# A logits stage reordered: the third user group alone for 11 strips, the two last groups together for 14, the last group alone for 11, with the last group's sums and dense pieces 39 blocks sooner

## The chip, the core and the metric

The program runs on one core of one Trainium2 chip. The metric is the device time of one execution in microseconds (us). One execution has also been recorded by the hardware profiler; its rows are shown below.

## What is computed

Embeddings of 200 items per user are pooled, 50 retrieved rows per user are averaged, both go through small dense layers, and the fused vector of each of the 1,024 users is multiplied with a projection of 12,500 items.

```python
seq_emb = jnp.where(mask, item_embeddings[clip(sequence_ids - 1, 0)], 0.0)
pooled = seq_emb.sum(axis=1) / denom
user_rep = pooled @ W_rec.T + b_rec                              # 512 wide
retrieved = item_embeddings[retrieved_indices].mean(axis=1)      # 50 rows of each user
gate = jax.nn.sigmoid(concat([user_rep, retrieved]) @ gate_W.T + gate_b)
fused = gate * user_rep + (1.0 - gate) * retrieved
logits = fused @ proj_W.T + proj_b                               # 1024 x 12500
```

## The kernel before, in words

**Groups, strips, blocks.** The 1,024 users are four groups (0 to 3) of 512, each four blocks of 128. The 12,500 items are NS = 25 strips of W = 500. A block of logits (128 users by 500 items) is made by `make_logits` with 12 matmuls (four of the hidden dimension's slices, times three products of high and low f16 parts), each 128 by 500, into one of BANKS = 5 banks. VectorE (DVE) evicts it at L955 into `rows` (the profile's `ring`), with the scale from `out_scale` and the bias; ScalarE (ACT) issues the store of every four blocks. `rows` holds three such sets of four.

**The logits stage.** It is a list STEPS of 400 blocks, and each engine walks through it in its own program order. A *turn* is one load of a strip. For each turn SyncE (SP) loads the strip (1 MB, `load_strip`) and its bias row spread over the partitions (`load_bias`, 250 KB), ACT makes the high part (`high_strip`, L1114), DVE the low part (`low_strip`, L772), and `scale_out` makes the combined scale (L780). Turns 0 to 24 use groups 0 and 1 (8 blocks a turn, 200 blocks). Turns 25 to 49 load all strips again for group 2 (4 blocks a turn, blocks 200 to 299), and turns 50 to 74 again for group 3 (blocks 300 to 399). TensorE (PE) waits for `strip_low` at the first block of a turn, and for `fused_low` of the group. A strip's squares and sum (L1105, L1316) and its scale are made once, in the first 25 turns. A turn's high and low parts are made at the turn before it: at its blocks 3 and 4 if that turn has 8 blocks, at its blocks 0 and 1 if it has 4.

**The dense work of groups 2 and 3** is threaded into the same walk by a table of block numbers, `LOGITS`. For a group there are `pool` (the pooled vector comes in and is split), 12 `pieces` on PE (four USER of 12 matmuls, L1238; four TURN, transposes of the retrieved means, L1256; four GATE of 24 matmuls), `square` and `sum` (a common scale), `high`, `low`, `diff`, `mix` (the gate is applied, in two steps at `mix` and `mix + 1`), `fsum` (the fused vector's scale; PE L1298) and `flow` (its low part, DVE L759, the last thing needed before the group's first logits).

**The gathers.** GpSimd (POOL) gathers the retrieved rows of 128 users with indirect DMAs (L560) into 11 slots of two gathers; DVE adds a slot's two gathers at L726 (`add_batch`), which frees the slot. There are 288 such adds, 114 before the logits stage. The other 174 are spread over blocks 5 to `ADDS_END` in proportion to PE's matmuls there (12 for a block, plus those of the dense pieces). When a block of users is summed POOL stores it (L565), and when all four of group 3 are there it loads them back for the transposes (`load_ret`, L614). TURN of group 3 waits for that load.

```python
block_work = accumulate(3 * KH + products(LOGITS, n) if n > LOGITS[1]["flow"] else 0 for n in range(ADDS_END + 1))
def adds_by_block(n):
    first, last = ADDS_PASS[NG - 1], len(pl.adds)
    return first if n < 0 else first + (last - first) * block_work[min(n, ADDS_END)] // block_work[-1]
```

Of the kernel before, what the change touches and what calls it, by code (L numbers as in the profile page):

```python
# [16 lines left out]
P = 128  # L17
# [15 lines left out]
ROWS = 4  # L33
# [27 lines left out]
    3: dict(pool=172, pieces=(174, 176, 178, 180, 256, 257, 258, 259, 269, 271, 273, 275), square=261, sum=263, high=264,  # L61
            low=266, diff=268, mix=277, fsum=283, flow=285),
# [9 lines left out]
ADDS_END = 246  # L72
# [72 lines left out]
def pooling_program(nc, pl, ids, ret_ids, emb, w_rec_t, b_rec, w_gate_t, b_gate, proj_t, proj_b,  # L145
# [9 lines left out]
    LAST = len(STEPS)  # L155

    def ended(t):

        return 1 + max(n for n, (turn, j) in enumerate(STEPS) if turn <= t)


    strip_steps = {"square": {9: 2}, "sum": {10: 2}, "high": {12: 2}, "low": {12: 2}}
    for t in range(3, TURNS):
        begun = STEPS.index((t - 1, 0))
        if t < NS:
            strip_steps["square"][begun] = t
            strip_steps["sum"][begun + 2] = t
# [3 lines left out]
    def group_of_step(t, j):  # L171
        return j // GROUP_BLOCKS if t < NS else t // NS + 1

    with ExitStack() as scope:
# [258 lines left out]
        def _(sp):  # L433
# [32 lines left out]
            def load_strip(t):  # L466
                c = t % NS
                if t >= 2:
                    sp.wait_ge(strip_low, t - 1)
                sp.dma_start(strip[:, t % 2], proj[:, :, c * W:(c + 1) * W]).then_inc(strip_in[t % 2], 16)  # L470

            def load_bias(t):
                c = t % NS
# [179 lines left out]
        def _(dve):  # L653
# [115 lines left out]
            def low_strip(t):  # L769
                c = t % NS  # L770
# [4 lines left out]
            def scale_out(t, groups=None):  # L775
                c = t % NS
                first, last = groups or ((0, 2) if t < NS else (t // NS + 1, t // NS + 2))
                at = first if t < NS else 0
# [165 lines left out]
            scale_out(0, (0, 1))  # L944
            scale_out(1, (0, 1))
            dve.drain()

            for n, (t, j) in enumerate(STEPS):
# [3 lines left out]
                if j == 0:  # L952
                    dve.wait_ge(bias_in[t % 2], 16 * (t // 2 + 1))
                dve.wait_ge(logits_made, n + 1)
                dve.scalar_tensor_tensor(rows[:, r % ROW_SLOTS, v], logit_ps[n % BANKS][:, 0:W],  # L955
                                         out_scale[:, t % 2, j // GROUP_BLOCKS:j // GROUP_BLOCKS + 1], bias[:, t % 2],
# [3 lines left out]
                if n in strip_steps["low"]:  # L960
                    made = strip_steps["low"][n]
                    low_strip(made)
                    if made % NS > 0:
                        scale_out(made)
                        dve.drain()
                dense_scales(n, LOGITS)
                dense_parts(n, LOGITS)
                if n == LOGITS[1]["flow"]:
                    scale_out(0, (1, 2))
                    scale_out(1, (1, 2))  # L970
# [3 lines left out]
                if t + 1 in (NS, 2 * NS) and n + 1 == ended(t):  # L974
                    dve.drain()
                    scale_out(t + 1)
                    dve.drain()
# [3 lines left out]
        def _(act):  # L981
# [126 lines left out]
            def high_strip(t):  # L1108
                c = t % NS
# [7 lines left out]
            def store_rows(r):  # L1117
                t, j = STEPS[r * ROWS]
                c = t % NS
                first = group_of_step(t, j) * GROUP_BLOCKS  # L1120
# [4 lines left out]
            def store_last_rows(v):  # L1125

                act.wait_ge(logits_moved, LAST - ROWS + v + 1)
                act.dma_start(out.rearrange("(b p) i -> p b i", p=P)[:, pl.blocks - ROWS + v, (NS - 1) * W:],
                             rows[:, (LAST // ROWS - 1) % ROW_SLOTS, v]).then_inc(last_stored, 16)

# [41 lines left out]
            for n, (t, j) in enumerate(STEPS):  # L1172
# [15 lines left out]
        def _(pe):  # L1188
# [130 lines left out]
            def make_logits(n):  # L1319
                t, j = STEPS[n]  # L1320
                g = group_of_step(t, j)
                if j == 0:
                    pe.wait_ge(strip_low, t + 1)
                if j % GROUP_BLOCKS == 0:
# [5 lines left out]
                at_user = (g % 2 * GROUP_BLOCKS + j % GROUP_BLOCKS) * P  # L1330
# [32 lines left out]
            for n, (t, j) in enumerate(STEPS):  # L1363
# [66 lines left out]
```

## Time and profile before

| | |
|---|---|
| device time, three runs | 2155.1, 2154.89, 2150.67 us; median 2154.89 |
| span of the profiled execution | 2152.5 us |
| PE, DVE, ACT, POOL busy over the span | 96%, 74%, 38%, 52% |
| stretch from 980 us to the end: PE idle | 10.3 of 1,172 us (1161.67 busy) |
| granted TensorE clock in that stretch | 1.00 |
| DMA share in 1600 to 1700 us, and in 2000 to 2100 us | 0.99 (356 GB/s), 0.68 (227 GB/s) |

No device time is given for the profiled execution by itself, only its span; the median of the runs is 2.4 us above it. Busy times are per engine. Idle time of an engine counts only where another waits for it. A "busy" of a stretch is the sum of the instructions' spans inside it. An ordinary gap between two DVE instructions (some 0.1 to 0.2 us) is not counted as busy.

### The profile page before, as it was taken

Reading aid. Unit: us, or ns where it says so; the run is one execution under the profiler, and the core shown is the slowest. Engines: PE = TensorE matmul, PEld = TensorE weight load, DVE = VectorE, ACT = ScalarE, POOL = GpSimd, SP = SyncE. Lnnn points to the kernel's source line nnn. Section 1 sums busy time; section 2 is a strip of 40 time slices with the busy share of each in tenths; the row PEclk is TensorE's granted clock in tenths of the full one; section 3 lists DMA queues with packets and bytes.
Section 4 is the critical chain, followed back from the end, with each engine's and each line's share of the span. In section 5 each row is a group of like instructions: output and inputs, shape, how many; then the busy total and the mean of one; then the engine's idle time right before and its main releaser. Section 6 shows DMA issues by size and latency. Waiting matters only on the chain.

```text
span 2152.5 us, 32020 instructions
## 1 busy us (share of the span) xinstructions
PE 2066.9 (96%) x12722; PEld 1060.7 (49%) x12722; DVE 1599.5 (74%) x1837; ACT 818.2 (38%) x1009; POOL 1117.7 (52%) x830
## 2 busy tenths in 40 slices
PE   5679999999999999999999999999999999999999
PEld 4555555555555554444444444444444444444444
DVE  8999999888888886444577787787878865655554
ACT  5866676444544455435211212232211222212111
POOL 5574552788678855656366666657667600000000
PEclk9559999999999999999999999999999999999999
DMA  8999997999899987979589998878899975566665
GB/s 300 339 230 302 289 324 253 308 250 258 240 272 246 250 296 254 322 245 330 176 281 335 317 307 300 297 266 267 318 318 350 370 237 170 196 223 235 229 218 187
DMA packets 222050, 586.82 MB, mean 273 GB/s; under 512 B 21840, under 2 KB 121040, under 8 KB 218576
## 3 DMA queue, kind: packets, MB, share of 16 engines
q1 hardware_dynamic: 91424, 264.21, 36.1%
q0 software_dynamic: 77632, 218.16, 35.8%
q10 hardware_dynamic: 52848, 102.41, 12.7%
q8 instruction: 103, 1.69, 0.3%
q14 instruction: 43, 0.35, 0.0%
HBM read 448.21 MB, written 136.48 MB: 272 GB/s over the span
## 4 chain that ended last, share of the span: by engine, by line
PE 85%; DVE 8%; ACT 3%; DVEq 1%; issue 1%; DMA 1%; another core or an unknown queue 0%; POOL 0%; ACTq 0%; SPq 0%; POOLq 0%
PE pooled_ps L1333 36%; PE pooled_ps L1226 27%; PE count_ps L1333 9%; PE count_ps L1208 7%; PE count_ps L1238 6%; DVE row_hots L681 2%; ACT counts L991 2%; DVE keys L683 2%; DVE recip L698 1%; ACT counts L985 1%; DMA mid<-emb 0%; DVEq L725 0%; DMA row_hots<-ret_dram 0%; DVE ring L688 0%; PE count_ps L1256 0%
## 5 line engine op out<-in xcount | busy, mean ns | idle before, releaser
L1226 PE MATMUL pooled_ps<-mid,ring 128*128 128x512 f16 x3136 | 725.4, 379 | 3.8 <-ACT mid L1009 1.9
L560 POOL DMA_INDIRECT gathered<-emb,ret_rows x460 | 556.1, 1209 | 308.4 <-DVE gathered L726 144.4
L1226 PEld LDWEIGHTS pooled_ps<-mid,ring 128*128 128x128 f16 x3136 | 292.3, 98 | 309.9 <-issue 4.5
L1333 PE MATMUL pooled_ps<-counts,mid 128*128 128x500 f16 x1920 | 413.0, 374 | 1.0 <-DVE counts L772 0.9
L1333 PE MATMUL pooled_ps<-counts,keys 128*128 128x500 f16 x1920 | 413.9, 374 | 0.0
L582 POOL DMA_INDIRECT gathered<-emb,ret_rows x184 | 342.4, 1861 | 132.7 <-ACT ring L999 56.3
L955 DVE SCALAR_TENSOR_TENSOR ring<-pooled_ps,out_scale,counts 128x500 f32<-128x500 f32 x320 | 234.3, 736 | 223.9 <-PE pooled_ps L1333 199.8
L681 DVE TENSOR_TENSOR row_hots<-pair_columns,keys 128x2048 f16<-128x2048 f16 x256 | 312.8, 1222 | 70.3 <-PE count_ps L1208 57.8
L1114 ACT ACTIVATE counts<-counts,strip_scale 128x2000 f16<-128x2000 f32 x75 | 147.0, 1960 | 509.2 <-PE pooled_ps L1333 291.3
L1208 PE MATMUL count_ps<-keys,row_hots 128*128 128x98 f16 x4096 | 280.5, 224 | 59.7 <-DVE keys L683 42.6
L1208 PEld LDWEIGHTS count_ps<-keys,row_hots 128*128 128x128 f16 x4096 | 250.1, 107 | 139.1 <-DVE keys L683 59.4
L985 ACT ACTIVATE counts<-count_ps 128x392 uint8<-128x392 f32 x512 | 237.9, 491 | 201.4 <-PE count_ps L1208 177.9
L1333 PEld LDWEIGHTS pooled_ps<-counts,mid 128*128 128x128 f16 x1920 | 186.6, 97 | 218.9 <-DVE counts L772 1.7
L1333 PEld LDWEIGHTS pooled_ps<-counts,keys 128*128 128x128 f16 x1920 | 185.1, 97 | 215.5
L1009 ACT ACTIVATE mid<-counts 128x1024 f16<-128x1024 uint8 x196 | 205.8, 1054 | 163.6 <-PE pooled_ps L1226 129.6
L683 DVE TENSOR_TENSOR keys<-pair_columns,keys 128x1568 f16<-128x1568 f16 x256 | 247.9, 968 | 0.0
L726 DVE TENSOR_TENSOR gathered<-gathered 128x1024 f32<-128x1024 f32 x159 | 195.0, 1226 | 57.9 <-issue 19.0
L772 DVE SCALAR_TENSOR_TENSOR counts<-counts,strip_scale 128x2000 f16<-128x2000 f32 x75 | 172.0, 2294 | 6.3 <-ACT counts L1114 6.3
L560 POOL DMA_INDIRECT counts<-emb,ret_rows x108 | 136.2, 1262 | 56.9 <-issue 30.2
L1333 PE MATMUL count_ps<-counts,keys 128*128 128x500 f16 x480 | 107.8, 374 | 0.0
L1333 PE MATMUL count_ps<-counts,mid 128*128 128x500 f16 x480 | 107.8, 374 | 0.0
L955 DVE SCALAR_TENSOR_TENSOR ring<-count_ps,out_scale,counts 128x500 f32<-128x500 f32 x80 | 58.9, 736 | 52.8 <-PE count_ps L1333 42.0
(134 smaller groups left out, 1110.6 us busy)
## 6 DMA issues: line engine op xcount, KB each, us to landing
logits<-ring ACTq DMA_DIRECT2D x99, 1000.0 KB
ring<-emb_parts SPq DMA_DIRECT2D x147, 512.0 KB
counts<-proj_t SPq DMA_DIRECT2D x75, 1000.0 KB
counts<-emb SPq DMA_DIRECT2D x14, 1792.0 KB, 10.9
emb_parts<-ring SPq DMA_DIRECT2D x49, 512.0 KB, 8.5
mid<-emb SPq DMA_DIRECT2D x46, 512.0 KB
counts<-proj_b SPq DMA_DIRECT2D x75, 250.0 KB
gathered<-emb,ret_rows POOLq DMA_INDIRECT x660
```

What stands on the lines that cost most here:

```text
L560: pool.indirect_dma_start(slots[group][:, a], None, source, column(block, r * SLOT + a))\
L582: pool.indirect_dma_start(to, None, source, column(block, n), compute_op=ALU.add).then_inc(landed, 16)
L681: dve.tensor_tensor(row_hots[:, n % 2], cols.broadcast_to((P, 8, P, 2)), rk.broadcast_to((P, 8, P, 2)), ALU.is_equal)
L683: dve.tensor_tensor(chunk_hots[:, n % 2], cols[:, :, 0:NQ].broadcast_to((P, 8, NQ, 2)), ck.broadcast_to((P, 8, NQ, 2)), ALU.is_equal).then ...
L726: dve.tensor_tensor(slots[total], slots[total], slots[more], ALU.add).then_inc(added, 1)
L772: dve.scalar_tensor_tensor(strip_parts[:, t % 2, 1], strip[:, t % 2], strip_scale[:, c:c + 1], strip_parts[:, t % 2, 0], ALU.mult, ALU.sub ...
L955: dve.scalar_tensor_tensor(rows[:, r % ROW_SLOTS, v], logit_ps[n % BANKS][:, 0:W], out_scale[:, t % 2, j // GROUP_BLOCKS:j // GROUP_BLOCKS ...
L985: act.activation(counts_v[:, g % 2, :, k * QUAD:(k + 1) * QUAD], count_ps[:, q % COUNT_BANKS, 0:QUAD * NQ].rearrange("p (u c) -> p c u", u ...
L1009: act.activation(cvt[:, p % CVT], counts_v[:, g % 2, 2 * i:2 * i + 2], ACT.Copy).then_inc(cvt_made, 1)
L1208: last = pe.matmul(to, row_hots[:, slot, pair * 2 + part, :, v], chunk_hots[:, slot, pair * 2 + part, :, v], start=(part == 0), stop=(part ...
L1226: last = pe.matmul(pooled_ps[:, m], ring_v[:, p % RING, c, part, m * P:(m + 1) * P], cvt[:, p % CVT, c], start=(i == 0 and c == 0 and part ...
L1333: last = pe.matmul(logit_ps[n % BANKS][:, 0:W], fused[g // 2][:, f, k, at_user:at_user + P], strip_parts[:, t % 2, w, k, :], start=(k == 0 ...
```

## The change

Group 3 no longer has 25 turns of its own behind those of group 2. Strips 0 to 10 are loaded for group 2 alone (11 turns of 4 blocks, blocks 200 to 243), strips 11 to 24 for groups 2 and 3 together (14 turns of 8 blocks, 244 to 355), and strips 0 to 10 again for group 3 alone (11 turns of 4 blocks, 356 to 399). There are 61 turns in place of 75, and still 400 blocks of 12 matmuls. The first block of group 3 is 248 in place of 300. So group 3's TURN and GATE pieces and everything behind them move 39 blocks to the front (`flow` from 285 to 246), its `pool` and USER pieces stay, and the adds end at block 207 in place of 246. `out_scale` of turn 36 for group 3 is made behind `flow`.

```diff
-    3: dict(pool=172, pieces=(174, 176, 178, 180, 256, 257, 258, 259, 269, 271, 273, 275), square=261, sum=263, high=264,
-            low=266, diff=268, mix=277, fsum=283, flow=285),
+    3: dict(pool=172, pieces=(174, 176, 178, 180, 217, 218, 219, 220, 230, 232, 234, 236), square=222, sum=224, high=225,
+            low=227, diff=229, mix=238, fsum=244, flow=246),
-ADDS_END = 246
+ADDS_END = 207
+ALONE = 11
-    TURNS = 3 * NS
-    STEPS = [(t, half * GROUP_BLOCKS + j) for half in range(2) for t in range(2) for j in range(GROUP_BLOCKS)]
-    STEPS += [(t, j) for t in range(2, TURNS) for j in range(2 * GROUP_BLOCKS if t < NS else GROUP_BLOCKS)]
+    LOADS = [(c, (0, 1)) for c in range(NS)] + [(c, (2,)) for c in range(ALONE)]
+    LOADS += [(c, (2, 3)) for c in range(ALONE, NS)] + [(c, (3,)) for c in range(ALONE)]
+    TURNS = len(LOADS)
+    STEPS = [(t, g, b) for g in range(2) for t in range(2) for b in range(GROUP_BLOCKS)]
+    STEPS += [(t, g, b) for t in range(2, TURNS) for g in LOADS[t][1] for b in range(GROUP_BLOCKS)]
...
-        strip_steps["high"][begun + (3 if t <= NS else 0)] = t
-        strip_steps["low"][begun + (4 if t <= NS else 1)] = t
+        wide = len(LOADS[t - 1][1]) > 1
+        strip_steps["high"][begun(t - 1) + (3 if wide else 0)] = t
+        strip_steps["low"][begun(t - 1) + (4 if wide else 1)] = t
...
-                    if made % NS > 0:
-                        scale_out(made)
-                        dve.drain()
+                    ready = [group for group in LOADS[made][1] if group == 0 or LOGITS[group]["flow"] < n]
+                    scale_out(made, ready[0], ready[-1] + 1)
+                    dve.drain()
...
+                if n == LOGITS[3]["flow"]:
+                    for made in range(NS, TURNS):
+                        if low_at[made] <= n < ended(made) and 3 in LOADS[made][1]:
+                            scale_out(made, 3, 4)
+                    dve.drain()
```

The rest of the diff carries the strip and the group of each step (`LOADS[t][0]`, `g`) into the loads, the stores, `high_strip`, `low_strip` and `make_logits`.

## Rows read from the trace of the kernel before

**Rows 1.** The page: busy time of each engine, share of the span, instructions.
```profile
PE 2066.9 (96%) x12722; PEld 1060.7 (49%) x12722; DVE 1599.5 (74%) x1837; ACT 818.2 (38%) x1009; POOL 1117.7 (52%) x830
```

**Rows 2.** Windows: length, busy us (count) of each engine, clock, DMA share, GB/s.
```profile
1130.00:1340.00 210.00, 210.00 (x1005) 96.81 (x1004) 165.32 (x249) 43.11 (x32) 138.11 (x120) 1.00 0.92 318
1380.00:1535.00 155.00, 152.98 (x738) 70.90 (x736) 124.33 (x184) 40.40 (x35) 104.91 (x88) 1.00 0.86 297
1600.00:1712.00 112.00, 112.00 (x533) 51.61 (x531) 91.75 (x95) 20.41 (x11) 83.09 (x63) 1.00 0.99 357
1870.00:2140.00 270.00, 270.00 (x1280) 124.46 (x1279) 144.24 (x161) 51.01 (x26) 0.00 (x0) 1.00 0.67 224
```

**Rows 3.** The chain that ended last: start, length, engine, tile, line, count.
```profile
1721.22 10.13 PE pooled_ps L1333 x48
...
2139.16 10.15 PE pooled_ps L1333 x48
```

**Rows 4.** Waits of PE from 980 us: us in total, times, longest.
```profile
PE count_ps L1238 <- DVE counts L801: 2.5, 2, 1.6
PE spare_ps L1316 <- issue: 1.4, 1, 1.4
PE count_ps L1238 <- DVE keys L823: 1.3, 1, 1.3
PE pooled_ps L1333 <- DVE counts L772: 0.9, 1, 0.9
...
PE count_ps L1256 <- DMA row_hots<-ret_dram: 0.7, 1, 0.7
```

**Rows 5.** Groups of instructions from 980 us: busy us, mean ns | idle before, releaser.
```profile
L955 DVE SCALAR_TENSOR_TENSOR ring<-pooled_ps,out_scale,counts 128x500 f32<-128x500 f32 x320 | 234.3, 736 | 223.9 <-PE pooled_ps L1333 199.8 <-issue 13.5 <-remote 7.0
...
L772 DVE SCALAR_TENSOR_TENSOR counts<-counts,strip_scale 128x2000 f16<-128x2000 f32 x75 | 172.0, 2294 | 6.3 <-ACT counts L1114 6.3
L1114 ACT ACTIVATE counts<-counts,strip_scale 128x2000 f16<-128x2000 f32 x75 | 147.0, 1960 | 509.2 <-PE pooled_ps L1333 291.3 <-issue 110.6 <-PE count_ps L1333 56.9
```

**Rows 6.** Timeline at the end of group 2's dense work: start, us, engine, line.
```profile
1491.50 0.16 PE L1316 MATMUL spare_ps<-strip_sq,ones_f 128*128 128x1 bf16 x1 [1.36 <-issue]
...
1501.99 2.29 DVE L772 SCALAR_TENSOR_TENSOR counts<-counts,strip_scale 128x2000 f16<-128x2000 f32 x1
1504.34 2.71 PE L1333 MATMUL count_ps<-counts,keys 128*128 128x500 f16 x12
```

**Rows 7.** POOL's groups in 1600 to 1712 us, columns as in rows 5.
```profile
L560 POOL DMA_INDIRECT gathered<-emb,ret_rows x38 | 49.5, 1302 | 17.4 <-issue 10.4 <-DVE gathered L726 7.0
L560 POOL DMA_INDIRECT counts<-emb,ret_rows x24 | 34.3, 1429 | 11.4 <-issue 7.0 <-DVE gathered L726 4.4
```

**Rows 8.** Timeline: last gather, last add, load of the sums, group 3's first TURN.
```profile
1710.52 1.06 POOL L560 DMA_INDIRECT counts<-emb,ret_rows  x1 [0.30 <-issue]
...
1739.29 1.22 DVE L726 TENSOR_TENSOR gathered<-gathered,counts 128x1024 f32<-128x1024 f32 x1
...
1745.72 0.56 POOL L614 DMA_DIRECT2D row_hots<-ret_dram  x1 [3.54 <-DMA ret_dram<-gathered]
...
1761.59 0.60 PE L1256 MATMUL count_ps<-identity,row_hots 128*128 128x128 f32 x4
```

**Rows 9.** Timeline from group 3's last GATE piece to its fused low part.
```profile
1834.78 10.30 PE L1333 MATMUL pooled_ps<-counts,mid 128*128 128x500 f16 x48
...
1837.62 0.74 DVE L955 SCALAR_TENSOR_TENSOR ring<-pooled_ps,out_scale,counts 128x500 f32<-128x500 f32 x1 [7.07 <-PE pooled_ps L1333]
...
1846.67 2.29 DVE L745 TENSOR_TENSOR counts<-counts 128x2048 f32<-128x2048 f32 x1
...
1849.00 1.91 ACT L1067 ACTIVATE counts<-counts 128x2048 f32<-128x2048 f32 x1 [11.39 <-DVE counts L745]
...
1852.89 2.30 DVE L772 SCALAR_TENSOR_TENSOR counts<-counts,strip_scale 128x2000 f16<-128x2000 f32 x1 [1.97 <-ACT counts L1114]
...
1865.45 2.35 DVE L759 SCALAR_TENSOR_TENSOR mid<-counts,fused_scale,mid 128x2048 f16<-128x2048 f32 x1
```

More of the change, by code:

```diff
@@ L150, in pooling_program, with begun @@
     GROUP_BLOCKS = G // P
-    TURNS = 3 * NS
-    STEPS = [(t, half * GROUP_BLOCKS + j) for half in range(2) for t in range(2) for j in range(GROUP_BLOCKS)]
-    STEPS += [(t, j) for t in range(2, TURNS) for j in range(2 * GROUP_BLOCKS if t < NS else GROUP_BLOCKS)]
+    LOADS = [(c, (0, 1)) for c in range(NS)] + [(c, (2,)) for c in range(ALONE)]
[3 more added lines that the diff above has]
+    STEPS += [(t, g, b) for t in range(2, TURNS) for g in LOADS[t][1] for b in range(GROUP_BLOCKS)]
     LAST = len(STEPS)
+    def begun(t):
+        return min(n for n, step in enumerate(STEPS) if step[0] == t)
     def ended(t):
-        return 1 + max(n for n, (turn, j) in enumerate(STEPS) if turn <= t)
+        return 1 + max(n for n, step in enumerate(STEPS) if step[0] <= t)
     strip_steps = {"square": {9: 2}, "sum": {10: 2}, "high": {12: 2}, "low": {12: 2}}
     for t in range(3, TURNS):
-        begun = STEPS.index((t - 1, 0))
         if t < NS:
-            strip_steps["square"][begun] = t
-            strip_steps["sum"][begun + 2] = t
-        strip_steps["high"][begun + (3 if t <= NS else 0)] = t
-        strip_steps["low"][begun + (4 if t <= NS else 1)] = t
-    def group_of_step(t, j):
-        return j // GROUP_BLOCKS if t < NS else t // NS + 1
+            strip_steps["square"][begun(t - 1)] = t
+            strip_steps["sum"][begun(t - 1) + 2] = t
+        wide = len(LOADS[t - 1][1]) > 1
+        strip_steps["high"][begun(t - 1) + (3 if wide else 0)] = t
+        strip_steps["low"][begun(t - 1) + (4 if wide else 1)] = t
+    low_at = {t: n for n, t in strip_steps["low"].items()}
     with ExitStack() as scope:
@@ L773, in low_strip, with scale_out @@
                                          strip_parts[:, t % 2, 0], ALU.mult, ALU.subtract).then_inc(strip_low, 1)
[L775 to L778, printed above, removed]
+            def scale_out(t, first, last):
+                c, at = LOADS[t][0], first - LOADS[t][1][0]
                 dve.drain()
@@ L943, in _ @@
             dve.drain()
-            scale_out(0, (0, 1))
-            scale_out(1, (0, 1))
+            scale_out(0, 0, 1)
+            scale_out(1, 0, 1)
             dve.drain()
-            for n, (t, j) in enumerate(STEPS):
+            for n, (t, g, b) in enumerate(STEPS):
                 r, v = divmod(n, ROWS)
@@ L955, in _ @@
                 dve.scalar_tensor_tensor(rows[:, r % ROW_SLOTS, v], logit_ps[n % BANKS][:, 0:W],
-                                         out_scale[:, t % 2, j // GROUP_BLOCKS:j // GROUP_BLOCKS + 1], bias[:, t % 2],
+                                         out_scale[:, t % 2, g - LOADS[t][1][0]:g - LOADS[t][1][0] + 1], bias[:, t % 2],
                                          ALU.mult, ALU.add).then_inc(logits_moved, 1)
@@ L968, in _ @@
                 if n == LOGITS[1]["flow"]:
-                    scale_out(0, (1, 2))
-                    scale_out(1, (1, 2))
+                    scale_out(0, 1, 2)
+                    scale_out(1, 1, 2)
+                    dve.drain()
[3 more added lines that the diff above has]
+                            scale_out(made, 3, 4)
                     dve.drain()
@@ L973, in _ @@
                     add_batch(k)
[L974 to L977, printed above, removed]
         @block0.scalar
@@ L1117, in store_rows @@
             def store_rows(r):
-                t, j = STEPS[r * ROWS]
-                c = t % NS
-                first = group_of_step(t, j) * GROUP_BLOCKS
+                t, g, b = STEPS[r * ROWS]
+                c = LOADS[t][0]
+                first = g * GROUP_BLOCKS
                 act.wait_ge(logits_moved, ROWS * (r + 1))
@@ L1127, in store_last_rows @@
                 act.wait_ge(logits_moved, LAST - ROWS + v + 1)
-                act.dma_start(out.rearrange("(b p) i -> p b i", p=P)[:, pl.blocks - ROWS + v, (NS - 1) * W:],
+                act.dma_start(out.rearrange("(b p) i -> p b i", p=P)[:, pl.blocks - ROWS + v, (ALONE - 1) * W:ALONE * W],
                              rows[:, (LAST // ROWS - 1) % ROW_SLOTS, v]).then_inc(last_stored, 16)
@@ L1171, in _ @@
                                 high_strip(c)
-            for n, (t, j) in enumerate(STEPS):
+            for n in range(LAST):
                 if n in strip_steps["square"]:
@@ L1362, in _ @@
                                 sum_strip(c)
-            for n, (t, j) in enumerate(STEPS):
+            for n in range(LAST):
                 make_logits(n)
```

19 lines of the change are left out of this document (9 added, 10 removed).

## The prediction

> **What bounds the kernel now.** I read the page first: PE is busy for 96% of the span, all others far less [rows 1]. That alone doesn't say that PE sets the end in the stage that is changed, so the windows come next. The granted clock is 1.00 in each, its upper level (2.4 GHz) [rows 2]. Read in them how PE's busy time stands to the length: 210.00 of 210, 112.00 of 112, 270.00 of 270 [rows 2]. The logits stage is matmuls back to back. The chain of waits says the same: it is PE L1333 in runs of 48 matmuls, 10.13 us for four blocks at 1721 us and 10.15 at the very end [rows 3]. One block is 2.53 us, one matmul 0.211. The two runs lie in different company, the first in the time of a DMA share near 0.99, the second at 0.67 [rows 2]. So a block costs the same under a full and under a half-empty DMA system. Last I read who makes PE wait: five lines, 6.8 us together [rows 4]. This is the whole of what any reordering of this stage can win, unless it removes matmuls. The change keeps 400 blocks of 12 and all 24 moved pieces.
>
> **What is taken away.** 14 turns go: each an `high_strip` on ACT (1.96 us), a `low_strip` on DVE (2.29), a small `scale_out`, a 1 MB load and a 250 KB bias. That is 27 us of ACT and 32 us of DVE [rows 5] and 17.5 MB. The cover is plain: in 1870 to 2140 us, with a turn every four blocks, DVE is busy for 144 us of 270 and ACT for 51, while PE is never idle [rows 2]. DVE waited for PE at the eviction for 199.8 us [rows 5]. The transfers are hidden as well, since a strip is asked for one turn and more ahead. Worth 0. All of this relief lies behind block 244; nothing of it helps the stretch ahead of it, which gets denser.
>
> **Adds closer together.** 174 adds are laid over PE's matmuls in blocks 5 to ADDS_END. Before: 242 blocks of 12, group 2's pieces 160, group 3's USER 48, 3,112 in all, or 17.9 matmuls an add, 3.77 us. After: 203 blocks, 2,644, or 15.2 matmuls, 3.21 us. Over 155 us that is 7.2 more adds, each 1.22 us [rows 8] and some 0.1 of gap, 9.5 us of DVE. In the densest stretch, 1380 to 1535, DVE is busy for 124.3 of 155 us [rows 2]; 30.7 are free, though some 18 of them are ordinary gaps between its 184 instructions. So DVE doesn't become the bound on average. Locally it does:
> - Group 2's end. L772 of block 156 ends at 1504.29 and PE's block 160 begins at 1504.34 [rows 6]: that low part is just in time. DVE has no rest between `mix` (147) and this point. By the formula of `adds_by_block` 6 adds stand in blocks 147 to 155 before, 7 after. One add more is 1.3 us of lateness, straight onto PE. It shows either at block 160 or already at block 154, where the strip's sum waits for `fused_scaled` for 1.36 us [rows 6], since that wait and the later one are on one DVE sequence: count it once. +1.3, bounds 0 (a gap takes it) and 2.6 (two adds).
> - Group 2's GATE at 139 waits for `both_low` in the same way: 3 adds in blocks 131 to 135 before, 4 after. The trace shows no wait there, but the margin is under a block. +0.3, bounds 0 and 1.3.
> - The TURN of group 2 waited 0.7 us for its rows [rows 4]. The adds that they need end at block 103 in place of 117, so this goes: -0.7.
>
> **The gathers.** They must all be in 39 blocks, 99 us, earlier. POOL now needs two per 3.21 us, 1.60 us each. In its slowest stretch 62 gathers took 83.8 us and 17.4 of issue, 1.63 us each, with 11.4 us of waiting for adds beside it [rows 7]; in 1130 to 1340 it is busy for 138 us with 120 instructions, 1.15 each, some 1.45 with the same 0.28 of issue [rows 2]. The slow stretch has the DMA share at 0.99, the other at 0.92. After the change all gathers lie in the cheaper kind but for the last few: with 8-block turns the strips, biases and stores are 3.33 MB in 20.3 us, 164 GB/s, and the gathers 0.524 MB in 3.21 us, 163 GB/s. 327 GB/s is asked where 357 were moved [rows 2]. POOL is then used to 90%. Its lead covers the rest: the last gather is issued at 1711.6 and the last add begins at 1739.3 [rows 8], 27.7 us. 0.
>
> The Trainium skill (DMA: Bandwidth & Descriptors, Specifications) gives a core some 358 GB/s of HBM bandwidth, which speaks against this packing. The slow stretch agrees with its 357. By that page the 8 blocks from 200 to 207, where short turns (227 GB/s) and gathers meet at 390, would fall behind by 32 GB/s for 20 us, 0.6 MB, an estimate of 2 us of transfer; as all of it is prefetch the sum would stay as it is.
>
> **Group 3's rows come back in time.** Add, store, load: 1739.3 to 1745.7, and PE's TURN at 1761.59 with no wait [rows 8, 4]. The last add (207) and the TURN (217) stay ten blocks apart. The store and the load stand last in POOL's queue, so nothing waits behind them. 15.3 us from the load's issue to the TURN held 1 MB under rising traffic; an add that is 3 us late changes nothing. 0.
>
> **Group 3's dense work.** It is the same chain with turn boundaries (multiples of 4) one block nearer. Before, `high_strip` stood behind `high_both` at block 264 and delayed `low_strip`: PE waited 0.9 for a strip and 1.3 for `both_low` [rows 4]. After, `high_strip` is at 224 and `high_both` at 225: both waits go, -2.2. What comes later is tighter, though. Take the start of the block behind the last GATE (276 before, 237 after) as zero. Before, evictions began at 2.84, the second mix at 11.9 and `square_fused` at 14.2, the strip's low part ended at 20.4, and its turn (284) began 8 blocks and a sum behind zero, 20.5 [rows 9]: in time by nothing. After: eviction 2.8 to 3.6, low part 5.9, first mix to 9.4, second to 12.8, `square_fused` to 15.0, high part 17.0, low part 19.3; but the turn (244) begins at 7 blocks, 17.7. PE waits 1.6. Then `fsum` at 244: PE ends that block at 21.9, eviction and scale to 24.6, high part 26.7, eviction 246 to 28.0, `low_fused` (2.35 us) to 30.4; block 248 can begin at 29.7. PE waits 0.7. Together +2.3, bounds 0 (DVE runs ahead) and 4.9, the case that `low_fused` ends 7.5 us behind its block as it does before (1867.8 [rows 9]; block 285 ends ten blocks and a sum behind zero, at 1860.3), with block 248 only 2.5 us away. Net with the two waits that go: +0.1.
>
> **Sum.** +1.3 +0.3 -0.7 +0.1 = +1.0 us. Span 2153.5; with the 2.4 us by which the median of the runs is above the span, 2155.9. I say 2156.
>
> **Rivals.**
> - DVE falls behind in group 2's stretch. For: DVE's small slack between blocks 131 and 160, and 7 adds more there. Against: it waits for PE again at several evictions, and five banks give 10 us. If the free time in 1380 to 1535 turned out to be all gaps, each added add would count in full: +9.5 us, 2164. It decides once DVE is late by four blocks, or a turn's low part by more than 3 us.
> - The gathers come late, and DVE stops in an add with evictions queued behind it. Each gather would have to cost over 1.60 + 27.7/348 = 1.68 us; the slowest stretch had 1.63. At 1.75 it is 348 times 0.07, +24 us: 2180.
> - The waits vanish: groups 2 and 3 both without a stall and none new. All 6.8 us won, 2148. Against: three of the five waits sit at places that the change leaves alone.
> - PE's matmuls get nearer together once DVE and DMA have less to do, that is behind block 244. At 1% of 156 blocks it would be 4 us, 2152 or below. Against: 10.13 and 10.15 us in unlike company. The Trainium skill (TensorE: Matmul & The Clock Gate, Back-to-back issue gap) has a sustained spacing of about 131 ns for 512 columns, by which 211 ns would not be PE's floor; this trace disagrees, with 48 matmuls in 10.13 us in every stretch.
> - The change doesn't do what it says: the turns do go, so it would be the gain that is absent, and this is my forecast.
>
> **How the numbers follow.** The forecast (small waits traded) 0.72; DVE short 0.13; gathers late 0.05; waits vanish 0.05; nearer matmuls 0.02; something not listed 0.03, taken as slower. 0.2% is 4.3 us, about what this kernel's runs differ by (2150.67 to 2155.1). The forecast's own bounds are 2153 to 2160 with unlike executions allowed for; 2159.2 is already "slower", some 0.01 of it, and as much goes to faster. Faster: the vanished waits 0.05, the nearer matmuls 0.02, a low draw of the forecast 0.01, together 0.08. Slower: DVE short 0.09 (its other 0.04 costs under 4 us), the late gathers 0.05, the unlisted 0.03, a high draw 0.01, together 0.18. Same: the rest, 0.74. The range is 2150 (half the waits won, low draws) to 2164 (DVE short in full); the late gathers and the full gain are left out.
>
> **What would show it.** Right: PE busy for all but some 10 us from 980 us on, still 10.13 us per four blocks, DVE busy for less behind block 244, POOL's last gather near 1612 us and the last add near 1640, and short waits at blocks 160, 244 and 248. Wrong: PE waits with `rows` or `logits_moved` behind it (an eviction, L955) between 1400 and 1520 us; DVE idle ahead of L726; a TURN at some 1663 us that waits for the load; a block that costs other than 2.53 us.

## The result and the profile after

The kernel with the change takes 2171.1 us (median of four runs, 2166.72 to 2173.71); the kernel before took 2152.78 beside it (four runs, 2149.57 to 2155.1). The ratio is 1.0085, 95% interval 1.0072 to 1.0097. It is some 18 us slower, and the forecast (2156, range 2150 to 2164) was wrong. The profiled execution has a span of 2170.2 us and a time of its own of 2171.93.

The page of the kernel after: busy time of each engine, and who sets the end, by engine. It answers to [rows 1].

```profile
PE 2072.6 (96%) x12722; PEld 1063.2 (49%) x12722; DVE 1564.4 (72%) x1810; ACT 789.9 (36%) x995; POOL 1156.2 (53%) x830
...
PE 53%; POOL 26%; DVE 7%; issue 6%; DMA 3%; ACT 3%; DVEq 1%; ACTq 0%; POOLq 0%; SPq 0%
```

PE's matmuls are the same 12,722, with 5.7 us more of busy time. DVE and ACT lose 35 and 28 us, as the 14 dropped turns should have it. POOL's 830 instructions are the same as before and take 38.5 us more. That is the first odd number: nothing in the diff makes a gather larger.

The end of the chain of waits after, and windows after (columns as in [rows 2]):

```profile
2156.78 10.15 PE pooled_ps L1338 x48
```

```profile
1300.00:1400.00 100.00, 90.74 (x418) 40.81 (x417) 73.64 (x103) 20.59 (x17) 81.10 (x65) 0.95 0.91 309
...
1500.00:1600.00 100.00, 91.92 (x426) 41.44 (x427) 77.34 (x107) 22.60 (x18) 78.87 (x64) 0.97 0.90 309
...
1900.00:2000.00 100.00, 100.00 (x476) 46.06 (x475) 41.30 (x50) 9.81 (x5) 0.00 (x0) 1.00 0.48 165
```

Four blocks still end in 10.15 us, as in [rows 3], and from 1900 to 2000 us PE is never idle at full clock while DVE is busy for 41 us and the DMA share is 0.48. The part that the change lightened costs what it did. Most of the loss lies in two hundreds, 1300 to 1400 and 1500 to 1600 us, where PE is idle for 9.3 and 8.1 us (before 2.3 and 0.9) and the clock's mean is below 1.

PE's waits after, from 980 us on (total, times, longest), against [rows 4]:

```profile
PE count_ps L1244 <- DVE counts L806: 14.0, 2, 8.4
PE pooled_ps L1338 <- DVE counts L779: 3.8, 4, 1.8
PE spare_ps L1322 <- DVEq L759: 2.1, 1, 2.1
PE spare_ps L1304 <- ACT counts L1073: 1.2, 2, 1.0
PE pooled_ps L1338 <- DVE mid L766: 0.6, 1, 0.6
...
PE count_ps L1262 <- DMA row_hots<-ret_dram: 0.4, 1, 0.4
```

(Lines are shifted: L801 of before is L806, L772 is L779, L1238 is L1244, L1333 is L1338, L955 is L960, L726 is L733, L560 is L567.) After, they sum to 22.1 us, of which the 0.4 for `row_hots` lies ahead of the logits stage. Before it is 7.7 and not the 6.8 of [rows 4], which leaves out two small ones:

```profile
PE count_ps L1238 <- issue: 0.7, 2, 0.4
...
PE spare_ps L1298 <- ACT counts L1067: 0.2, 1, 0.2
```

Two of the waits after make 14.0: the first USER piece of group 2 (block 110) and that of group 3 (block 174) wait for the low part of the pooled vector, L806, for 8.42 and 5.60 us. Ahead of the result that line was only the largest of PE's small waits. Of the 3.8 us at L779, 3.0 are low parts of strips that are late in the same way (at 1323, 1536 and 1666 us), and they are gone where the gathers are healed, in the run with one input below; 0.8 are at block 244.

Each of the two idle times at L806 is followed by a second cost. PE in the timeline after, the same piece of group 2 before, and the windows of the two pieces after:

```profile
1349.59 5.28 PE L1244 MATMUL count_ps<-counts 128*128 128x512 f16 x12 [8.42 <-DVE counts L806]
...
1559.33 4.91 PE L1244 MATMUL count_ps<-counts 128*128 128x512 f16 x12 [5.60 <-DVE counts L806]
```

```profile
1344.57 2.75 PE L1238 MATMUL count_ps<-counts 128*128 128x512 f16 x12 [1.61 <-DVE counts L801]
```

```profile
1349.60:1354.80 5.20, 5.20 (x13) 1.84 (x14) 4.90 (x5) 0.00 (x0) 4.29 (x5) 0.50 0.90 297
1559.40:1564.10 4.70, 4.70 (x13) 1.66 (x14) 4.52 (x5) 0.00 (x0) 3.62 (x4) 0.54 0.88 309
```

The granted clock is 0.50 and 0.54 over these pieces, so 1.2 GHz, its lower level, for nearly all of them; twelve such matmuls take 5.28 and 4.91 us where the piece before, at 2.4 GHz, took 2.75. That is 4.7 us for both.

**The account.** The stage goes from the first block (1049.35 before, 1047.63 after) to the end of the last four (2139.16 + 10.15 and 2156.78 + 10.15). Its windows, before and after:

```profile
1049.35:2149.31 1099.96, 1092.32 (x5199) 503.40 (x5197) 756.46 (x979) 236.87 (x168) 435.62 (x363) 1.00 0.79 270
```

```profile
1047.63:2166.93 1119.30, 1097.45 (x5199) 504.45 (x5197) 720.06 (x951) 209.63 (x154) 470.34 (x363) 0.99 0.73 249
```

It is 19.3 us longer: PE is idle for 14.2 us more (21.85 for 7.64), and busy for 5.1 more, of which the two slow pieces are 4.7. The stage began 1.7 us sooner, which leaves +17.7 on the span.

**Why the low part is late.** What DVE waits for in 1100 to 1660 us, DMA rows only:

```profile
DVE gathered L733 <- DMA gathered<-emb,ret_rows: 18.0, 16, 2.4
...
DVE gathered L733 <- DMA counts<-emb,ret_rows: 7.3, 5, 3.9
...
DVE counts L733 <- DMA counts<-emb,ret_rows: 4.4, 2, 3.7
...
DVE counts L733 <- DMA gathered<-emb,ret_rows: 1.8, 2, 1.0
```

The adds stop for gathered rows for 31.5 us, and everything behind them in DVE's queue stops with them. Around block 109 DVE's evictions are 12.2 us behind PE's blocks. PE bridges that as long as a bank is free; a low part in the same queue has no such cushion. So the gathers come late. POOL's groups in 1100 to 1600 us, after and then before:

```profile
L567 POOL DMA_INDIRECT gathered<-emb,ret_rows x215 | 280.9, 1307 | 66.7 <-issue 64.3 <-DMA ret_dram<-gathered 2.1 <-DVE counts L733 0.3
L567 POOL DMA_INDIRECT counts<-emb,ret_rows x90 | 119.5, 1327 | 30.0 <-issue 26.8 <-DMA ret_dram<-counts 2.9 <-DVE counts L733 0.3
```

```profile
L560 POOL DMA_INDIRECT gathered<-emb,ret_rows x196 | 234.0, 1194 | 122.9 <-issue 49.6 <-DVE gathered L726 44.4 <-DVE counts L726 27.8
L560 POOL DMA_INDIRECT counts<-emb,ret_rows x78 | 96.3, 1234 | 43.7 <-issue 21.3 <-DVE gathered L726 16.4 <-DVE counts L726 6.0
```

Before, POOL waits for adds for 94.6 us of these 500 (44.4 + 27.8 + 16.4 + 6.0): it is ahead and is held back. After, it waits for them for 0.6 us. It issues without a rest, 305 gathers in 280.9 + 119.5 + 66.7 + 30.0 = 497.1 us, or 1.63 us each. POOL is busy for 53% of the span on the page and for 400.4 us of these 500, and is their bound all the same: nearly all of the rest is the 0.30 us of issue between two gathers.

**What makes a gather dear** shows in the timeline, POOL and DVE together:

```profile
1335.86 0.95 POOL L567 DMA_INDIRECT gathered<-emb,ret_rows  x1 [0.30 <-issue]
1336.72 1.22 DVE L733 TENSOR_TENSOR counts<-counts 128x1024 f32<-128x1024 f32 x1 [3.65 <-DMA counts<-emb,ret_rows]
1337.11 1.65 POOL L567 DMA_INDIRECT gathered<-emb,ret_rows  x1 [0.30 <-issue]
...
1340.32 0.95 POOL L567 DMA_INDIRECT gathered<-emb,ret_rows  x1 [0.30 <-issue]
...
1340.64 1.22 DVE L733 TENSOR_TENSOR counts<-counts,gathered 128x1024 f32<-128x1024 f32 x1 [0.18 <-issue]
...
1344.40 2.29 DVE L779 SCALAR_TENSOR_TENSOR counts<-counts,strip_scale 128x2000 f16<-128x2000 f32 x1
1344.96 2.55 POOL L567 DMA_INDIRECT counts<-emb,ret_rows  x1 [0.30 <-issue]
...
1347.09 2.35 DVE L806 SCALAR_TENSOR_TENSOR counts<-counts,small 128x2048 f16<-128x2048 f32 x1
1347.81 2.44 POOL L567 DMA_INDIRECT counts<-emb,ret_rows  x1 [0.30 <-issue]
```

A gather takes 0.95 us while DVE waits. One that begins while an add is running (1337.11) ends 0.82 us behind the add's end, and takes 1.65; one that is already under way when the add begins (1340.32) still takes 0.95. Those that begin under the two low parts take 2.55 and 2.44. Add and low part are DVE instructions that read two inputs from SBUF.

The trace of 1100 to 1600 us says the same of all gathers, once the start of each is laid over these DVE instructions. Of 304 gathers 177 begin while one runs; they take 1.58 us in the mean, and 166 of them end 0.8 us behind it. The other 127 take 0.95, none over 1.0. Among these are 45 that begin during an eviction, which reads one input from SBUF and writes 500 columns. Before, 110 of 273 begin under a two-input instruction, again at 1.58 us, and the other 163 take 0.95. Call such a gather caught: its price didn't change; the share of caught ones did, from 40% to 58%. Two things go with it. The adds come every 3.21 us in place of 3.77. And POOL no longer waits: before, 52 gathers had waited for an add to free their slot, so that they began behind its end, and 2 of them were caught; of the other 221 it was 49%.

**How much was asked of POOL.** Here the working before the result has a miscount, and the section on the gathers ahead of it has it too. An add doesn't join the two gathers of a slot: it adds a slot of two rows to the total, and 50 rows are 25 slots and 24 adds, the first slot being the total itself. (That section also says 1,024 users; there are 2,048, four groups of 512, and the 288 adds are those of 12 blocks of 128.) The 174 adds need 174 × 25/24 × 2 = 362 gathers (359 of them are in the trace after), not 348. So the pace asked is 3.21/2.083 = 1.54 us a gather, not 1.60. At 1087 to 1260 us the trace has 104 gathers, 1.66 us each, where 112 were due: four slots short. Counted back from the last gather and the last add, POOL's lead is 7 slots at 1087 us and between 2 and 3 at 1260 (within a slot, since a few records are missing); before, it is between 6 and 9 all the way. From then on the adds wait.

### The profile page after: what moved, and what is told of

It is laid out like the page before. It is cut to its first block, busy times and chain, and to the rows that moved or that the text cites. A ratio compares the mean times of both kernels' runs of the same rounds, so it can differ in the third digit from the quotient of the medians.

```text
span 2170.2 us, 31909 instructions
## 1 busy us (share of the span) xinstructions
PE 2072.6 (96%) x12722; PEld 1063.2 (49%) x12722; DVE 1564.4 (72%) x1810; ACT 789.9 (36%) x995; POOL 1156.2 (53%) x830
## 4 chain that ended last, share of the span: by engine, by line
PE 53%; POOL 26%; DVE 7%; issue 6%; DMA 3%; ACT 3%; DVEq 1%; ACTq 0%; POOLq 0%; SPq 0%
PE pooled_ps L1232 22%; PE pooled_ps L1338 17%; POOL gathered L567 16%; POOL counts L567 6%; PE count_ps L1214 6%; PE count_ps L1338 4%; POOL gathered L589 3%; PE count_ps L1244 3%; ACT counts L997 2%; DVE row_hots L688 2%; DVE keys L690 1%; DMA ret_dram<-gathered 1%; DMA counts<-pool_dram 1%; ACT counts L991 1%; DMA ret_dram<-counts 0%
## 5 line engine op out<-in xcount | busy, mean ns | idle before, releaser
L567 POOL DMA_INDIRECT gathered<-emb,ret_rows x460 | 585.1, 1272 | 239.2 <-issue 133.2
L589 POOL DMA_INDIRECT gathered<-emb,ret_rows x184 | 349.7, 1901 | 127.5 <-ACT ring L1005 55.3
L1338 PE MATMUL pooled_ps<-counts,keys 128*128 128x500 f16 x1920 | 414.8, 374 | 2.6 <-DVE counts L779 2.6
L1338 PE MATMUL pooled_ps<-counts,mid 128*128 128x500 f16 x1920 | 413.0, 374 | 1.8 <-DVE counts L779 1.2
L960 DVE SCALAR_TENSOR_TENSOR ring<-pooled_ps,out_scale,counts 128x500 f32<-128x500 f32 x320 | 235.0, 736 | 244.0 <-PE pooled_ps L1338 241.2
L1120 ACT ACTIVATE counts<-counts,strip_scale 128x2000 f16<-128x2000 f32 x61 | 119.6, 1960 | 574.4 <-DVE ring L960 242.7
L1338 PEld LDWEIGHTS pooled_ps<-counts,mid 128*128 128x128 f16 x1920 | 186.6, 97 | 220.5 <-DVE counts L779 2.2
L1338 PEld LDWEIGHTS pooled_ps<-counts,keys 128*128 128x128 f16 x1920 | 185.2, 97 | 219.2 <-DVE counts L779 3.6
L733 DVE TENSOR_TENSOR gathered<-gathered 128x1024 f32<-128x1024 f32 x159 | 194.9, 1226 | 69.0 <-PE pooled_ps L1232 35.9
L567 POOL DMA_INDIRECT counts<-emb,ret_rows x108 | 141.8, 1313 | 35.5 <-issue 32.3
L779 DVE SCALAR_TENSOR_TENSOR counts<-counts,strip_scale 128x2000 f16<-128x2000 f32 x61 | 139.9, 2294 | 5.0 <-ACT counts L1120 2.6
L1338 PE MATMUL count_ps<-counts,keys 128*128 128x500 f16 x480 | 107.8, 374 | 0.1
L1338 PE MATMUL count_ps<-counts,mid 128*128 128x500 f16 x480 | 107.8, 374 | 0.0
L1244 PE MATMUL count_ps<-counts 128*128 128x512 f16 x384 | 92.4, 393 | 14.0 <-DVE counts L806 14.0
```

The costliest lines, as they stand in the source:

```text
L567: pool.indirect_dma_start(slots[group][:, a], None, source, column(block, r * SLOT + a))\
L589: pool.indirect_dma_start(to, None, source, column(block, n), compute_op=ALU.add).then_inc(landed, 16)
L733: dve.tensor_tensor(slots[total], slots[total], slots[more], ALU.add).then_inc(added, 1)
L1244: done = pe.matmul(to, weights[:, w, k, m * P:(m + 1) * P], x, start=(first and k == 0 and at == 0), stop=(last and k == KH - 1 and at == 2))
L1338: last = pe.matmul(logit_ps[n % BANKS][:, 0:W], fused[g // 2][:, f, k, at_user:at_user + P], strip_parts[:, t % 2, w, k, :], start=(k == 0 ...
```

## Experiments

The kernels named below are the kernel before or after with one edit. Expectations were written ahead of the runs and go by the miscounted paces: their 1.60, 1.75 and 1.66 us a gather (11, 16 and 13 strips alone) are 1.54, 1.68 and 1.60 by the right count.

### The adds sooner, nothing else

The kernel before, with its own order and table.

```diff
-ADDS_END = 246
+ADDS_END = 207
```

> The kernel before with one number changed: the adds end at block 207 in place of 246. Steps, turns and dense table are those of before. Theory G (POOL can't gather at the asked pace of one per 1.60 us, so adds wait for rows, and DVE comes late to group 2's and 3's low_pool): the cost is nearly all there, 12 to 20 us over before, with PE waiting for low_pool (L801) for 10 us or more, as in the changed kernel (14.0). Rival O (the new order of turns or the moved dense table costs the time): within 3 us of before.

Measured: 2171.64 us (four runs, 2169.02 to 2177.4), 20.3 above the kernel before beside it, ratio 1.0099, interval 1.0082 to 1.0116. PE's largest wait:

```profile
PE count_ps L1238 <- DVE counts L801: 13.7, 2, 7.5
```

One number makes the whole loss, with the same wait, 13.7 us for 14.0. POOL's gathers are at 1.29 and 1.32 us and wait 0.3 us for an add in 500.

### The order, nothing else

Against the kernel before (cut):

```diff
+ALONE = 21
...
+    LOADS = [(c, (0, 1)) for c in range(NS)] + [(c, (2,)) for c in range(ALONE)]
+    LOADS += [(c, (2, 3)) for c in range(ALONE, NS)] + [(c, (3,)) for c in range(ALONE)]
```

The rest of the change is kept; `LOGITS` and `ADDS_END` are those of before, for which group 3 may begin behind strip 21 at the soonest.

> The new order of turns with the dense table and ADDS_END of before: group 2 alone for 21 strips, both for 4, group 3 alone for 21 (first block of group 3 is 288, flow stays 285). Theory G: the time of before within 3 us, PE waits under 10 us in all. Rival O: slower by 5 us or more, with PE waits behind block 284.

Measured: 2152.11 us (ten runs, 2150.18 to 2152.64), ratio 1.0002, interval 0.9993 to 1.0012. POOL waits for adds for 94 us again, and PE's waits sum to 6.4. The order costs and brings nothing.

### Adds with one input from SBUF

The test of the mechanism: the kernel after, with the 174 adds replaced by an instruction of the same length that reads the new slot alone and writes two columns. It leaves out the sums of the retrieved rows; the waits, slots and gathers stay.

```diff
-                dve.tensor_tensor(slots[total], slots[total], slots[more], ALU.add).then_inc(added, 1)
+                if k < ADDS_PASS[3]:
+                    dve.tensor_tensor(slots[total], slots[total], slots[more], ALU.add).then_inc(added, 1)
+                else:
+                    dve.tensor_reduce(slots[total][:, :, 0], slots[more], AX.X, ALU.add).then_inc(added, 1)
```

> The changed kernel, where the 174 adds of the logits stage are replaced by a tensor_reduce over the newly gathered slot alone, about 1.1 us long as the add is (1.22), but with one SBUF input in place of two; so the retrieved sums of groups 2 and 3 are left out. Waits, slots and gathers stay. Theory G with its cause (a gather's descriptors wait while DVE runs an instruction with two SBUF inputs): gathers get shorter, from a mean of 1.31 us to 1.15 or less, POOL waits for adds again, and the time is within 4 us of before. Rival D (bandwidth, or POOL's own pace): gathers keep their mean of 1.3 us and the time stays at 2165 or more.

Measured: 2153.16 us (ten runs, 2150.51 to 2155.23), ratio 1.0006, interval 0.9997 to 1.0016. Its groups in 1100 to 1600 us (L736 is the stand-in here), its window, and behind it that window of the kernel after:

```profile
L567 POOL DMA_INDIRECT gathered<-emb,ret_rows x227 | 246.7, 1087 | 102.9 <-issue 59.8 <-DVE gathered L736 25.6 <-DVE counts L736 15.3
...
L736 DVE TENSOR_REDUCE gathered<-gathered 128x2 f32<-128x1024 f32 x71 | 86.7, 1222 | 8.0 <-issue 2.4
```

```profile
1100.00:1600.00 500.00, 493.62 (x2361) 227.49 (x2360) 416.52 (x586) 113.47 (x94) 354.52 (x331) 1.00 0.92 328
```

```profile
1100.00:1600.00 500.00, 480.13 (x2271) 219.83 (x2269) 399.36 (x562) 110.31 (x92) 403.64 (x313) 0.98 0.91 312
```

The stand-in takes 1222 ns, as the adds do (1225). The order, the table and the pace are those of the change. DVE is busy for longer than in the kernel after (416.52 us for 399.36) and the DMA engines move more (328 GB/s for 312). The second input is gone, and with it the loss: a gather takes 1.09 us, POOL waits for adds again (58.5 us), and 323 gathers in 500 us are 1.55 us each, which is the pace asked. PE's waits are 7.9 us. So it is neither DVE's load nor the memory's, and not the moved dense work either.

The edit takes away most of what an add writes as well (2 columns for 1,024). That this is not the cause is seen beside it: the 45 gathers that begin during an eviction, with one input from SBUF and 500 columns written, take 0.95 us in the kernel after. The 117 that begin under a stand-in take 0.95 too, where one that began under an add took up to 2 us. In this kernel 34 of 322 gathers are still caught, by the low parts and the other two-input instructions of the dense work.

The Trainium skill (SBUF — State Buffer, "SBUF: two separate sides" and "Who interferes with whom") has a DVE instruction with two SBUF inputs contend with a GpSimd instruction that reads SBUF, and one with a single SBUF input, outside the 2-port modes, not. The trace and this run agree, with 1.31 against 1.09 us. The Trainium skill adds, in the second of these sections, that in a probe `tensor_tensor` didn't stall a DMA; for these indirect gathers the timeline above disagrees (1.65 us for one that begins under an add, 0.95 without).

### Half of the stores' traffic

The rival that memory traffic slows the gathers. The kernel after, with half of each row of logits left unstored (but for the last four blocks).

```diff
-                act.dma_start(out.rearrange("(b p) i -> p b i", p=P)[:, first:first + ROWS, c * W:(c + 1) * W],
-                             rows[:, r % ROW_SLOTS]).then_inc(rows_stored[r % ROW_SLOTS], 16)
+                act.dma_start(out.rearrange("(b p) i -> p b i", p=P)[:, first:first + ROWS, c * W:c * W + W // 2],
+                             rows[:, r % ROW_SLOTS, :, 0:W // 2]).then_inc(rows_stored[r % ROW_SLOTS], 16)
```

> The changed kernel, where each store of four blocks of logits but the last carries the first 250 of its 500 columns (the others are left out), so that in the 8-block turns some 50 GB/s of some 325 go. All instructions stay. Theory G with its cause: the gathers' mean stays near 1.3 us and the time near that of the changed kernel, 2165 or more. Rival D (DMA bandwidth makes the gathers late): the waits of the adds shrink and the time goes to 2158 or less.

Measured: 2166.61 us (four runs, 2163.51 to 2168.01), ratio 1.0069, interval 1.0054 to 1.0083. In 1100 to 1600 us:

```profile
L567 POOL DMA_INDIRECT gathered<-emb,ret_rows x217 | 283.9, 1308 | 66.1 <-issue 66.1
```

```profile
1100.00:1600.00 500.00, 487.84 (x2312) 223.80 (x2311) 406.27 (x576) 111.50 (x93) 406.36 (x315) 0.99 0.86 271
```

271 GB/s in place of 312, and a gather still takes 1308 ns (1307). Traffic isn't what makes issue dear. Beside its own kernel before it is 14.8 us slower, where the change was 18.3; the two intervals overlap, so some 3.5 us may have gone. What the trace does show is a shorter time from issue to landing. The last figure of a row is its median in us, in 1100 to 1600 us, first after, then here:

```profile
gathered<-emb,ret_rows POOLq DMA_INDIRECT x215, 6.0
```

```profile
gathered<-emb,ret_rows POOLq DMA_INDIRECT x217, 5.1
```

With a small lead the adds wait for landings, so this may be what gave the time back; no run sets it apart. It is not what healed the kernel with one input, where the median is 6.1.

### The pooled vector's parts sooner

The rival that the two low parts are only placed too late. The kernel after:

```diff
-    2: dict(pool=108, pieces=(110, 112, 114, 116, 126, 127, 128, 129, 139, 141, 143, 145), square=130, sum=132, high=133,
+    2: dict(pool=98, pieces=(110, 112, 114, 116, 126, 127, 128, 129, 139, 141, 143, 145), square=130, sum=132, high=133,
-    3: dict(pool=172, pieces=(174, 176, 178, 180, 217, 218, 219, 220, 230, 232, 234, 236), square=222, sum=224, high=225,
+    3: dict(pool=167, pieces=(174, 176, 178, 180, 217, 218, 219, 220, 230, 232, 234, 236), square=222, sum=224, high=225,
```

> The changed kernel with low_pool and high_pool of group 2 at block 98 in place of 108 and of group 3 at 167 in place of 172; the USER pieces stay. Theory G: POOL sets the pace, so the wait only moves: L806 no longer holds PE, but PE then waits at evictions or at group 3's TURN, and 8 us or more over before remain (of 18). Rival L (it is only that low_pool stands too near to its pieces): the time goes to within 4 us of before.

Measured: 2171.53 us (four runs, 2167.96 to 2175.53), ratio 1.0084, interval 1.0067 to 1.0101. Nothing is won. PE's largest waits, and DVE's for rows:

```profile
PE pooled_ps L1338 <- DVE counts L779: 10.9, 6, 3.5
...
PE spare_ps L1297 <- DVEq L774: 4.4, 1, 4.4
```

```profile
DVE gathered L733 <- DMA gathered<-emb,ret_rows: 34.5, 22, 5.6
```

The wait at the low part of the pooled vector is gone, and the strips' low parts (L779) take its place, not the evictions or group 3's TURN that were expected. The adds wait for rows for 68.8 us in all instead of 31.5 (1100 to 1660 us), and some other low part is late. The likely reason is that PE's long stop had let the gathers catch up; this was not tested by itself. Whoever reads only PE's waits mends the place, not the shortage.

### The same edit on the kernel before

```diff
-    2: dict(pool=108, pieces=(110, 112, 114, 116, 126, 127, 128, 129, 139, 141, 143, 145), square=130, sum=132, high=133,
+    2: dict(pool=104, pieces=(110, 112, 114, 116, 126, 127, 128, 129, 139, 141, 143, 145), square=130, sum=132, high=133,
-    3: dict(pool=172, pieces=(174, 176, 178, 180, 256, 257, 258, 259, 269, 271, 273, 275), square=261, sum=263, high=264,
+    3: dict(pool=169, pieces=(174, 176, 178, 180, 256, 257, 258, 259, 269, 271, 273, 275), square=261, sum=263, high=264,
```

> The kernel before with low_pool and high_pool of group 2 at block 104 in place of 108 and of group 3 at 169 in place of 172, the pieces where they are. The gathers have slack there, so PE's two waits for L801 (2.5 us) go: 1 to 3 us faster, at the edge of what can be measured. If the waits turn up elsewhere: no change.

Measured: 2147.8 us (eleven runs, 2145.53 to 2151.24), ratio 0.9981, interval 0.9972 to 0.999. Its waits of PE:

```profile
PE spare_ps L1316 <- DVEq L752: 1.4, 1, 1.4
PE count_ps L1238 <- DVE keys L823: 1.3, 1, 1.3
PE pooled_ps L1333 <- DVE counts L772: 0.9, 1, 0.9
PE spare_ps L1298 <- ACT counts L1067: 0.2, 1, 0.2
```

Where POOL has its lead the same cure works: the 2.5 us at L801 of [rows 4] are gone and not replaced. A small win, 4.0 us below the kernel before beside it, and its interval holds it apart from no change.

### 16 and 13 strips alone

How tight may it be? The kernel after, with less moved to the front: group 3's table from its TURN on is 20 or 8 blocks later than in the kernel after (the table's lines are left out of the cuts below).

```diff
-ADDS_END = 207
+ADDS_END = 227
...
-ALONE = 11
+ALONE = 16
```

> Half the shift: group 2 alone for 16 strips, both groups for 9, group 3 alone for 16; group 3's later entries of the dense table 20 blocks later than in the changed kernel (flow 266, first block 268), the adds end at block 227. They then come one per 16.6 matmuls, 3.50 us, 1.75 us a gather. Theory G: POOL manages 1.6, so the gathers keep up: within 3 us of before. Rival N (the loss grows with each block of shift, by half here): 2160 to 2163.

Measured: 2150.01 us (twelve runs, 2147.77 to 2157.74), ratio 0.9997, interval 0.9989 to 1.0006. 298 gathers in 1100 to 1600 us, 1.68 each: the pace asked. POOL waits for adds for 39.7 us.

```diff
-ADDS_END = 207
+ADDS_END = 215
...
-ALONE = 11
+ALONE = 13
```

> Group 2 alone for 13 strips, both for 12, group 3 alone for 13; dense table 8 blocks later than in the changed kernel, the adds end at block 215: one per 15.7 matmuls, 3.32 us, 1.66 us a gather. POOL manages about 1.6 without waits for adds, and a little more time with the stores of sums. Theory G: POOL hardly waits for adds and just keeps up, 0 to 4 us over before. Rival N (a loss in proportion to the shift, 18 us by 39 blocks): 14 us over.

Measured: 2154.98 us (eleven runs, 2153.57 to 2160.09), ratio 1.0017, interval 1.0007 to 1.0026. 307 gathers in the 500 us, 1.63 each where 1.60 is asked; POOL hardly waits for an add (4 us), its lead is down to some 5 slots at 1600 us and holds until the end. (The profiled execution, 2160.09 us, is the slowest of the eleven; from 980 us on PE is idle for 11.3 us in it, before 10.3, so what it took above the median lies mostly ahead of the stage.) The edge lies between this kernel and the one with the change: +0.17% at 1.60, +0.85% at 1.54.

### 16 strips alone, parts sooner

The 16-strip kernel with the pool table's 104 and 169 of the edit above.

> The half shift (16, 9, 16 strips, adds to block 227) with low_pool of group 2 at block 104 and of group 3 at 169. Theory: the 1.8 us of waits for L806 go, as in the kernel before with the same edit, so 2147 to 2149, and no more than that kernel, since PE has nothing else to win from the order. If the new order has a gain of its own: 2 us or more below the kernel before with the same edit.

Measured: 2147.24 us (eleven runs, 2145.28 to 2153.93), ratio 0.9985, interval 0.9976 to 0.9994. The fastest median, but beside the kernel before with the same edit (0.9981, 0.9972 to 0.999) there is no difference. Even where POOL keeps up the new order is worth nothing.

## Why the prediction was wrong

**The step that failed** is the gathers': "POOL is then used to 90%. Its lead covers the rest", 0. It failed in three numbers.
- The pace: 348 gathers at 1.60 us. There are 362, at 1.54.
- The price: 1.45 us, worked out from 1130 to 1340 us of [rows 2]. That mean belongs to adds 3.77 us apart and to a POOL that often waits for them; 38% of its gathers begin under a two-input DVE instruction. Under the change it is 62% and 1.66 us while the lead is drained, and 58% and 1.63 over the 500 us, almost exactly the 1.63 that the slow stretch of [rows 7] had shown. I had put that stretch's price down to its DMA share of 0.99. Its trace says otherwise: 32 of 61 gathers are caught there, at 1.71 us, since with 4-block turns there are 10 low parts of 2.29 us beside 29 adds in 112 us (11 beside 55 in the 210 us from 1130 on); the other 29 take 0.95 at that DMA share too.
- The point from which it decides: 1.60 + 27.7/348 = 1.68, "the slowest stretch had 1.63". With the right count it is 1.54 + 27.7/362 = 1.62, so 1.63 is beyond it. The rival that was given 0.05 should have been near even, and by the price of 1.63 it was the likelier case.

**The rival "gathers come late"** is what happened, and its shape was right in half: DVE does stop in an add with evictions queued behind. Its price of +24 us went by a last add that is late for group 3. In fact the TURN of group 3, at 1681.42 us, doesn't wait for its rows at all. The cost arises 107 and 43 blocks ahead of that TURN (217), where PE needs a low part that stands behind the stopped adds, and a third of the idle time comes again as a lower clock (4.7 us for 14.0). I had priced no idle time with its clock.

**The rival "DVE falls behind"** came near the place (a turn's low part more than 3 us late; it was the pooled vector's), but for a cause that isn't there. With the one-input stand-in DVE is busier and in time.

**What held.** The removed turns are worth 0: 10.15 us for four blocks at half the DMA share, and the order alone is at 1.0002. Group 3's dense chain: forecast waits of 1.6 us at block 244 and 0.7 at 248, measured 0.8 (L779) and 0.6 (L766); the two old ones at its strip and at `both_low` (L823) are gone. Group 2's 0.7 at its TURN is gone, as forecast. Its sum at block 154: 1.36 to 2.1 us, and its `fsum` 0.2 to 1.0, forecast +1.3 for block 154 and block 160 together. The kernel with the gathers healed stands 1.84 us above the kernel before, where the sum said +1.0. So the other terms together were right within 1 us, as far as that kernel's interval (0.9997 to 1.0016) can tell, and the one was worth the whole result. The 2.4 us from span to time were 1.7 in the profiled execution (2171.93 for 2170.2).

**What was to show it** did: "DVE idle ahead of L726" came true, as did a last gather far behind the forecast. End of the queue, after (here L736 is the last step of a block's sum):

```profile
1652.59 2.55 POOL L567 DMA_INDIRECT counts<-emb,ret_rows  x1 [0.30 <-issue]
...
1662.95 0.58 POOL L572 DMA_DIRECT2D ret_dram<-gathered  x1 [7.80 <-DVE gathered L736]
...
1667.16 0.56 POOL L621 DMA_DIRECT2D row_hots<-ret_dram  x1 [3.63 <-DMA ret_dram<-gathered]
```

The last gather is at 1652.6 in place of the 1612 forecast, and 58 us sooner than before, not 99.

## What to carry to other kernels

- A mean price taken at one density doesn't hold at another when the price depends on who is active beside it. Split the group by what runs when each one begins (here 0.95 free, 1.58 caught) before multiplying. A stretch in which the engine waits shows too low a mean: before, the gathers that had waited took 0.96, the others 1.26.
- An engine that waits for its consumer in the profile (POOL, 94.6 us of 500) has at most that much reserve, less what its instructions gain in length. Count the work from the loop's own numbers, 25 slots for 24 adds: at 1.63 us a gather these 4% are the difference between "covered" and "short".
- If a producer is short, moving the wait's victim only moves the wait. Look for the queue in which the victim stands and what stops that queue.

## What the hardware showed that I had not expected

- An indirect gather of 128 rows of 2 KB takes POOL 0.95 us and 0.30 of issue. If it begins while a DVE instruction with two SBUF inputs runs, it ends some 0.8 us behind that one's end: 1.58 us in the mean, 2.55 under a low part of 2.29. If it is already under way, it takes 0.95 all the same (61 gathers of the trace after). With one input in the add, the mean of all is 1.09.
- After 8.42 and 5.60 us of idle time the clock is at 0.50 and 0.54 over PE's next 12 matmuls, at a cost of 2.5 and 2.2 us.
- A matmul of 500 columns is 211 ns (10.13 to 10.15 us for 48) in the stretch with a DMA share of 0.99 as in the emptier ones, down to 0.48.

Open: what in the gather the DVE instruction holds up (its read of the row numbers or the writing of its descriptors) was not taken apart; and whether the sooner landings account for what half of the stores' traffic gave back.
